# Zero fills, a branch of TensorE, and the order of the score groups in a hybrid attention kernel

## The reference

```python
x = x + attn_a(layernorm(x))   # softmax attention, 16 heads of 8, causal, bias slope[h] * min(k - q, 0)
x = x + ffn(layernorm(x))      # token shift, two mixes, relu squared, sigmoid gate
x = x + attn_b(layernorm(x))   # linear attention with rotary positions
x = x + ffn(layernorm(x))

attn = einsum('bhqd,bhkd->bhqk', Q, K) / sqrt(HD)
attn = where(causal, attn + slopes[:, None, None] * rel, -inf)
out  = einsum('bhqk,bhkd->bhqd', softmax(attn), V) @ W_O.T
```

## Time and profile before

| | us |
|---|---|
| median of 3 runs | 380.14 (379.83 to 380.43) |
| the profiled execution, its own time | 380.15 |
| its span, first to last instruction | 378.4 |
| TensorE busy | 330.1 (87%) |
| ScalarE busy | 293.8 (78%) |
| VectorE busy | 169.4 (45%) |
| GpSimd busy | 62.6 (17%) |
| first score product of the attention starts at | 47.59 |
| last exponential of the attention ends at | 290.8 |

### The profile page before, as it was taken

The page is one execution under the profiler, slowest core; times in us unless marked ns, Lnnn a source line. Parts: engine busy times, 40 slices in busy tenths (PEclk is TensorE's granted clock), DMA queues, the critical chain, the costliest instruction groups (busy, mean ns, idle before and its releaser), DMA issues.

```text
span 378.4 us, 6520 instructions
## 1 busy us (share of the span) xinstructions
PE 330.1 (87%) x2540; PEld 149.6 (40%) x2540; DVE 169.4 (45%) x400; ACT 293.8 (78%) x425; POOL 62.6 (17%) x63
## 2 busy tenths in 40 slices
PE   4814879999999999999999999999999988878795
PEld 2403522323332332322332233223323856868674
DVE  6897511424332422322300331022202779996965
ACT  5201368999999999998899989998999576983771
POOL 8795000003000000000000000000000253720340
PEclk9985958999999999999999999999999999999998
DMA  6220145666400000000000000000001100000002
GB/s 222 58 88 28 60 155 156 194 190 199 136 0 2 0 3 2 0 2 0 2 2 0 3 0 2 0 2 2 0 3 56 57 2 1 3 0 2 1 29 83
DMA packets 13268, 16.47 MB, mean 44 GB/s; under 512 B 1489, under 2 KB 8017, under 8 KB 13137
## 3 DMA queue, kind: packets, MB, share of 16 engines
q1 hardware_dynamic: 13232, 16.01, 13.6%
HBM read 6.56 MB, written 2.62 MB: 24 GB/s over the span
## 4 chain that ended last, share of the span: by engine, by line
PE 57%; DVE 17%; ACT 17%; issue 7%; POOL 1%; DMA 1%; DVEq 0%; ACTq 0%; POOLq 0%
PE ps L998 24%; PE ps L977 17%; ACT probs L488 10%; ACT x L488 5%; DVE probs L264 5%; PE ps L830 4%; PE ps L1007 2%; PE ps L1058 2%; PE ps L843 2%; DVE stats L563 2%; PE ps L825 2%; DVE scr L771 1%; ACT scr L497 1%; DVE ot L685 1%; POOL rstd L412 1%
## 5 line engine op out<-in xcount | busy, mean ns | idle before, releaser
L488 ACT ACTIVATE probs<-ps 128x1024 f32<-128x1024 f32 (+8 forms) x220 | 172.4, 870 | 18.8 <-PE ps L977 17.3
L977 PE MATMUL ps<-qr,kr 64*128 64x512 f32 (+7 forms) x592 | 109.7, 423 | 10.1 <-ACT probs L488 7.3
L998 PE MATMUL ps<-probs,vaug 128*9 128x512 f32 (+9 forms) x880 | 101.3, 509 | 1.0 <-DVE ot L685 0.7
L977 PEld LDWEIGHTS ps<-qr,kr 64*128 64x128 f32 x592 | 49.8, 187 | 117.7 <-ACT probs L488 66.8
L710 DVE TENSOR_TENSOR probs<-probs,cs 128x512 f32<-128x512 f32 x51 | 35.2, 691 | 79.8 <-ACT probs L488 79.8
L488 ACT ACTIVATE x<-ps 128x1024 f32<-128x1024 f32 (+5 forms) x76 | 62.3, 872 | 2.3 <-PE ps L977 2.1
L412 POOL TENSOR_TENSOR rstd<-veps,neghalf 128x4 f32<-128x4 f32 x16 | 17.0, 1064 | 240.9 <-DVE veps L569 240.8
L830 PE MATMUL ps<-w,scr 128*128 128x128 f32 x288 | 35.6, 277 | 2.1 <-DVE scr L773 1.6
L830 PEld LDWEIGHTS ps<-w,scr 128*128 128x128 f32 x288 | 33.9, 192 | 6.2 <-issue 4.3
L998 PE MATMUL ps<-x,vaug 128*9 128x512 f32 (+4 forms) x304 | 34.6, 521 | 0.0
L685 DVE COPY ot<-ps 128x512 f32<-128x512 f32 x16 | 11.1, 691 | 45.8 <-PE ps L998 45.6
(11 more groups left out here) (98 smaller groups left out, 266.1 us busy)
## 6 DMA issues: line engine op xcount, KB each, us to landing
x<-in_x SPq DMA_DIRECT2D x8, 256.0 KB, 4.2
qr<-parts_mid SPq DMA_DIRECT2D x16, 128.0 KB, 2.9
kr<-parts_mid SPq DMA_DIRECT2D x16, 128.0 KB, 3.0
kr<-att SPq DMA_DIRECT2D x8, 128.0 KB, 2.6
qr<-att SPq DMA_DIRECT2D x8, 128.0 KB, 3.2
qr<-parts_last SPq DMA_DIRECT2D x8, 128.0 KB, 3.6
kr<-parts_last SPq DMA_DIRECT2D x8, 128.0 KB, 3.2
out_y<-x SPq DMA_DIRECT2D x4, 256.0 KB, 2.3
```

Of the source, the lines that this page charges most:

```text
L488: nc.scalar.activation(slot[:, 2 * u:2 * u + 2, w0:w1], ps[:, b:b + 2, w0:w1], ACT.Exp).then_inc(exp_done, 1)
L977: ins = nc.tensor.matmul(ps[:, 2 * (n % 3) + v, w0:w1], kr[kb // TPC][a:a + SIDE, j, P * (kb % TPC):P * (kb % TPC + 1)], qr[unit.c][a:a + ...
L998: ins = nc.tensor.matmul(ps[32 * v:32 * v + V1, 6 + unit.lane, w0:w1], vaug[:, kb, V1 * h:V1 * (h + 1)], probs_slot(unit)[:, v, w0:w1], st ...
```

## The change

1. **Zeros.** ScalarE now fills the first half of `qr[1]` too, right behind `kr[0]`. GpSimd fills the other half, and everything else but `kr[1]`, only after DVE has applied the layernorm of slice 2 (`ln1_ready[2]`). SyncE waits for each half by its side.
2. **The first slice.** TensorE turns slice 0 before `gram_products`; `fourth_powers` moves behind the first queries and keys, `sum_of_heads` behind the keys of slice 1. DVE takes the statistics of slices 1 and 2 before `bound(0)`, those of slice 3 behind the first low halves, and `bound(2)` behind its second apply. The warm-up has one product, not two.
3. **Values.** ScalarE takes the values of slices 0 and 2.
4. **The branch.** TensorE reads the flag after slice 2, and `keep_clock` runs 4 products instead of 8, twice. The usual path is now the code right behind TensorE's branch, and the code of the attention and of what follows it, up to slice 3 of the third layernorm, stands a second time in the other block. The two blocks share the code from `turn_ln3(NCH - 1)` on. In `in_turn` the queries and keys of slice 2 now come ahead of `turn_ln3(3)`. SyncE waits for TensorE's `branched` alone.
5. **Groups.** `ORDER` has each group alone, in lane 0.
6. **Constants.** `constant_rows(1, 0)` is issued behind the first three `product_rows`, not ahead of them.

```diff
-WARM_UP = 2
-KEEP = 8
+WARM_UP = 1
+KEEP = 4
...
-        ORDER = (((1, 1), None), ((1, 2), None), ((1, 3), (0, 0)), ((2, 1), (0, 1)), ((2, 2), (0, 2)), ((2, 3), (0, 3)),
-                 ((3, 1), (1, 0)), ((3, 2), (2, 0)), ((3, 3), (3, 0)))
+        ORDER = [((c, g), None) for c, g in ((1, 1), (1, 2), (1, 3), (0, 0), (0, 1), (0, 2), (0, 3), (1, 0), (2, 1), (2, 2), (2, 3),
+                                             (2, 0), (3, 1), (3, 2), (3, 0), (3, 3))]
...
-            for n, m in FIRST:
-                constant_rows(n, m)
+            for n in range(2):
+                constant_rows(n, 1)
             for n, m in FIRST:
                 product_rows(n, m, 0)
-            sp.wait_ge(branched, 2)
+            constant_rows(1, 0)
+            sp.wait_ge(branched, 1)
...
                 rstd_of(LN1, n)
-                if n == 0:
-                    nc.gpsimd.memset(qr[1].bitcast(F32)[:, :, :], 0.0).then_inc(zeroed, 1)
                 if n % 2:
                     ln_apply(nc.gpsimd, pool, LN1, n, xh_a[:, cols(n)])
+            pool.wait_ge(ln1_ready[2], 1)
+            nc.gpsimd.memset(qr[1].bitcast(F32)[:, PAIRS // 2:, :], 0.0).then_inc(zeroed, 1)
             nc.gpsimd.memset(far[:], 0.0).then_inc(pool_ready, 1)
...
-            nc.scalar.activation(kr[0][:, :, :].rearrange("p j t -> p (j t)"),
-                                 neghalf[:, 0:1].broadcast_to([P, PAIRS * CH]), ACT.Copy, scale=0.0).then_inc(first_zeroed, 1)
+            for z, pairs in ((kr[0], PAIRS), (qr[1], PAIRS // 2)):
+                nc.scalar.activation(z[:, 0:pairs, :].rearrange("p j t -> p (j t)"),
+                                     neghalf[:, 0:1].broadcast_to([P, pairs * CH]), ACT.Copy, scale=0.0).then_inc(first_zeroed, 1)
...
                 if n:
                     take_high(n, 1)
+                if n % 2 == 0:
+                    take_values(n)
...
-            for n in range(1, NCH):
-                ln1_stats(n)
-                bound(n - 1)
+            ln1_stats(1)
+            ln1_stats(2)
+            bound(0)
             for s in range(2):
                 low_half(0, s)
+            ln1_stats(3)
+            bound(1)
             ln1_apply(2)
-            take_values(0)
+            bound(2)
             for n in range(1, NCH):
                 low_half(n, 0)
                 low_half(n, 1)
-                take_values(n)
+                if n % 2:
+                    take_values(n)
...
+            turn_ln1(0)
             gram_products()
-            turn_ln1(0)
-            fourth_powers()
             for n in range(NCH):
                 query_or_key(n, 0)
                 if n:
                     turn_ahead(n)
                 query_or_key(n, 1)
                 if n == 0:
+                    fourth_powers()
+                    turn_ahead(n)
+                if n == 1:
                     sum_of_heads()
-                    turn_ahead(n)
                 values(n)
-
-            pe.wait_ge(cb_loaded, 16)
+                if n == NCH - 2:
+                    pe.wait_ge(cb_loaded, 16)
+                    pe.wait_ge(flag_ready, 1)
+                    small = pe.value_load(flag[0:1, 0:1], min_val=0, max_val=1)
             keep_clock(KEEP, 0)
-            pe.wait_ge(flag_ready, 1)
-            small = pe.value_load(flag[0:1, 0:1], min_val=0, max_val=1)
-            with pe.If(small == 0):
+            def larger_scores():
...
+                in_turn(but_first(turn_ln2), but_first(lambda n: mix_k_in(0, n)), lambda n: mix_rv(0, n), None, None, but_last(turn_ln3),
+                        but_last(lambda n: (q_b(n), k_b(n))))
+            with pe.If(small == 1):
+                attention_and_more()
+            with pe.If(small == 0):
+                larger_scores()
+                attention_and_more()
+            turn_ln3(NCH - 1)
+            q_b(NCH - 1)
+            k_b(NCH - 1)
```

83 lines of the change are left out of this document (48 added, 35 removed).

## The result

The changed kernel took 366.46 us (median of 4 executions, 364.77 to 369.90); the kernel before took 380.28 in the same session (4 executions, 379.83 to 383.71). The ratio is 0.963, with a 95% interval of 0.953 to 0.973. The forecast was 359.9 us with a range of 356.0 to 365.5: the direction held, the size did not, and the time lies above the range.

A forecast was written before the change was run, and what follows sets the result against it. It blamed GpSimd's fills holding DVE's apply of slice 2 in the opening, with TensorE and ScalarE both full in the attention. Terms -18.9 - 1.4 - 1.0 + 0.5 - 0.6 + 1.1 = -20.3 from 380.15 gave 359.9 us, range 356.0 to 365.5.

The forecast's parts named there:

- From the apply of slice 2 to the first score: Opening: 13.8 us before, forecast 11.2 as the later of two paths plus 0.3, first score at 28.6.
- The tail: After the attention: TensorE's new jump ahead of turn_ln3(3) costs +1.1 us (0.3 to 4).
- The order: Attention: each group alone instead of mixed costs +0.5 us, bounds -2 to +4.3.
- The 18.9 us: Opening: first score product 18.9 us earlier (16.6 to 21), at 28.6 instead of 47.59.
- path by the rows: Apply to first score: low half after 3.9 us, SyncE's issues near 4, landing 3.0, together 10.9 us.
- path by TensorE's own work: Apply to first score: 13.8 us less clock, fillers and branch hole, plus bound and values copy, 10.7 us.
- The rule weighed: Branch and tail jump: a taken branch outside fetched code stalls; both holes go and return at the jump, shifting 0.8 us.
- The low clock in the first units: First eight units of the attention: half of 1.9 us lost at the lower clock returns, -1.0 us (-1.9 to +2).
- rival (d): Tail jump bites twice: holes of 1.6 and 1.7, then lower clock, +4 instead of +1.1, 362.8 us; chance 0.09.
- (b): Opening: the flag's instruction L604 waits for a GpSimd fill of 3.5 us, giving 363.4 us; chance 0.10.
- (c): Opening: fills hold all of DVE's work, first score at 38, time 369 us; chance 0.04.
- Rival (a): Attention: groups bound by TensorE, order costs +4.3 instead of +0.5, 363.7 us; chance 0.16.

The follow-up runs named there:

- before_third: Kernel of before, no edit, profiled in its short course: 362.46 us; the session's others took 364.16 and, four of them, 379.42 to 383.59.
- before_again: Kernel of before, no edit, profiled again: 381.19 us (3 executions, 380.17 to 381.66), all long.
- b_fills_wait: Kernel of before with GpSimd's memset of `far` and all behind it waiting for the apply of slice 2: 364.18 us (12 executions).
- a_mixed_units: Changed kernel with `ORDER` as in the kernel of before: 364.72 us (362.86 to 367.40, 12 executions).
- a_four_edits: Changed kernel with constant rows in the middle, order of before, jump inside the wait and eight fillers ahead of the jump: 361.13 us (6 executions).
- second trace of the same kernel: Changed kernel once more, no edit: 366.62 us (364.91 to 369.76, 11 executions), the profiled one 367.00.

## Why before has two courses

**Before again, twice.** No edit.

> The kernel of before once more, for a trace of its other course. In 34 further executions it took 361.8 to 366.0 us in 20 and 379.0 to 381.9 us in 14, and nothing between; the trace that the prediction rests on is of one at 380.15. Theory one (VectorE's apply of slice 2 is held, or not): in an execution near 363.5 us that apply, 14.91 us for four instructions beside GpSimd's 6.97 us memset, takes 1.1 us as VectorE's apply of slice 0 does without a memset beside it or up to 7.5 us, the first score comes 14 to 18 us earlier than 47.59 us, and everything from the second group on has the lengths of the trace of before. Theory two (something else differs, such as a transfer that lands late or the clock): the apply takes 14.9 us there too and the time is lost elsewhere.

Measured: 381.19 us (3 executions, 380.17 to 381.66), all long. For the four instructions of the apply of slice 2 the trace gives the duration (ns, shortest/median/longest) and the start of the first and the last, and then DVE's and GpSimd's timelines read:

```profile
L264 DVE TENSOR_SCALAR probs<-x,negmean,rstd x4: 328/7524/15041, 18.3 to 33.5; 128x128 f32<-128x128 f32 x4
```

```profile
18.27 15.61 DVE L264 TENSOR_SCALAR probs<-x,negmean,rstd 128x128 f32<-128x128 f32 x4
```

```profile
18.61 0.82 POOL L434 MEMSET far<- 128x864 f32 x1
```

The first instruction takes 15.04 us, from 18.27 to 33.31; the second stands behind it and ends with it; the last two take 0.33 each. GpSimd's memset of `far` starts at 18.61, and four fills of 3.5 us follow without a gap, up to 33.2. The prediction had the instructions let in one by one between two fills. They are not: the first waits for all five memsets. By these rows its start lies 0.34 us ahead of the first memset, in the trace of the prediction 0.37 behind it (18.85 against 18.48), and it is held in both.

> The kernel of before again, since the trace taken last fell in its long course too (381.19 us, the apply of slice 2 held from 18.27 to 33.88 us, GpSimd's memset of the tile far beginning at 18.61). Theory one (the apply is caught by the memsets, or gets through ahead of them): in an execution near 363.5 us the apply begins at 17.5 us or earlier, takes 1.1 us and is over when that memset begins; the first score stands 14 to 18 us earlier than 47.59. The rest has the lengths that the trace at 380.15 us shows. Theory two: the apply begins as late as in the long course and is not held, so what holds it is something else.

Measured: one execution at 362.46 us, which was the profiled one, one at 364.16, four from 379.42 to 383.59. The short course on DVE and on GpSimd:

```profile
15.39 0.27 DVE L603 TENSOR_REDUCE largest<-ps 1x1 f32<-1x128 f32 x1
15.70 0.14 DVE L604 TENSOR_SCALAR flag<-largest 1x1 int32<-1x1 f32 x1
15.77 1.27 DVE L581 SCALAR_TENSOR_TENSOR att<-ps,att 128x512 f32<-128x512 f32 x2
16.96 1.09 DVE L264 TENSOR_SCALAR probs<-x,negmean,rstd 128x128 f32<-128x128 f32 x4
```

```profile
18.59 0.81 POOL L434 MEMSET far<- 128x864 f32 x1
```

The apply is over at 18.05, half a us ahead of the memset. In the long course it began at 18.85, 0.4 us after it. What made it 1.9 us later is TensorE. First the short course (`before_third`), then the long one of the profile before:

```profile
12.58 1.88 PE L843 MATMUL ps<-probs,w 128*128 128x512 f32 x4
14.39 0.38 PE L863 MATMUL ps<-cs,fourth 128*1 128x128 f32 x2
```

```profile
13.10 3.62 PE L843 MATMUL ps<-probs,w 128*128 128x512 f32 x4
16.65 0.58 PE L863 MATMUL ps<-cs,fourth 128*1 128x128 f32 x2
```

The same four products take 1.88 us or 3.62 (592 ns each or 1061), the full or the half level. The sum over heads behind them, which DVE's reduction and all behind it wait for, starts at 14.4 or at 16.65. (The clock's column says 1.00 for both: no change is on record until 11.3 and 17.8 us, and only the durations tell which level the start has. The other long trace, `before_again`, has a record: the half level from 12.28 to 15.70 us, and the sum at 16.27.)

**More or less work for TensorE at the start.**

```
-WARM_UP = 2
+WARM_UP = 4
```

> The kernel of before with four products of 384 columns in TensorE's opening in place of two. Theory one (which course an execution of before takes is decided by when TensorE's clock has risen: in the short one the four products of query and key of slices 0 take 592 ns each and the sum over heads starts by 14.7 us, in the long one 1061 ns each and it starts at 16.3 to 16.7, so the apply of slice 2 comes 1.3 to 1.9 us later and meets GpSimd's memset): two more products, 1.3 us at the half level, fill the 0.9 us that TensorE idles at 9.4 us, the clock rises by 11.5 us in nearly every execution and nearly all take the short course, 362 to 366 us. Theory two (the course is decided by the arrival of the weights or of x): about half stay near 380 us.

Measured: 365.13 us (363.54 to 367.89), 12 executions, none long; 1.0036 of the short course (1.0003 to 1.0069). The four products take 1.88 us at 12.86, and the apply begins at 17.25.

```
-WARM_UP = 2
+WARM_UP = 0
```

> The kernel of before without those two products, the opposite step. Theory one (the clock decides the course): TensorE has done less by 11 us, the clock rises late, the four query and key products take 1061 ns each, and nearly all executions take the long course, 379 to 384 us. Theory two: about half stay near 363.5 us. A third outcome would be that the products start 1 us earlier without the two ahead of them, and enough so that even at the half level the sum over heads is there in time; then nearly all are short and the clock is right only in part.

Measured: 380.48 us (378.61 to 382.32), 6 executions, all long. TensorE's timeline shows the four products at 13.05 taking 3.62 us, and DVE's apply 14.48 us from 18.71. In the same session 15 executions of before were short and 8 long. Theory one in both: the level that the clock has during these four products decides the course.

**GpSimd's later fills wait.**

```
+            pool.wait_ge(ln1_ready[2], 1)
             nc.gpsimd.memset(far[:], 0.0).then_inc(pool_ready, 1)
```

> The kernel of before with one wait added on GpSimd: the memset of the tile far and all behind it begin only after VectorE's apply of slice 2, the early fill of query slice 1 stays where it was. Nothing on VectorE or TensorE changes. Theory one (the long course is that apply caught by these memsets and nothing else; the clock only sets when it begins): the apply takes 1.1 us in either clock, no execution near 380 us is left, those with the late clock end 1 to 2 us above the others, and all lie between 361.5 and 367 us. Theory two (a late clock costs the 16 us in another way): a part stays near 380 us. Beside the kernel whose fill of slice 1 waited as well (370.69 us) this one tells what that fill's lateness cost: some 6 us.

Measured: 364.18 us (362.25 to 366.91), 12 executions, none long. With the fills away from the apply nothing else remains of the 16 us.

**The apply ahead of the bound's wait.**

```
             for n in range(1, NCH):
                 ln1_stats(n)
+                if n == NCH - 1:
+                    ln1_apply(2)
                 bound(n - 1)
...
-            ln1_apply(2)
             take_values(0)
```

> The kernel of before with one edit on VectorE: the apply of slice 2 stands ahead of the step that waits for TensorE's sum over heads (and of the flag and the two low halves), as in the changed kernel, and no longer behind them; GpSimd's fills stay where they were. Theory one (the long course is this apply caught by the memsets that begin at 18.5 us): it begins at about 15.7 us and ends by 17, so no execution near 380 us is left, and the times are those of before's short ones, 362 to 365 us. Theory two (GpSimd's memsets hold whatever VectorE runs beside them): a part of the executions stays long.

Measured: 364.30 us (361.55 to 366.38), 12 executions, none long. The apply runs from 15.66 for 1.12 us. In the profiled execution the four products took 3.62 us, so the clock was late there and the course short all the same (363.5 us of span): for the long course the clock matters only through the moment of the apply. Either edit alone takes the long course away at no cost to the short one (ratios 1.0001, 0.9975 to 1.0027, and 1.0006, 0.9970 to 1.0043). The changed kernel pays 0.8% for the same.

**GpSimd's fill of query slice 1 late as well.**

```
-                if n == 0:
-                    nc.gpsimd.memset(qr[1].bitcast(F32)[:, :, :], 0.0).then_inc(zeroed, 1)
...
+            pool.wait_ge(ln1_ready[2], 1)
+            nc.gpsimd.memset(qr[1].bitcast(F32)[:, :, :], 0.0).then_inc(zeroed, 1)
             nc.gpsimd.memset(far[:], 0.0).then_inc(pool_ready, 1)
```

> The kernel of before with one edit: GpSimd fills query slice 1 with zeros only after VectorE has applied the normalisation to slice 2 (in the changed kernel GpSimd's half of it waits for the same). Theory one (the long executions of before are those in which the apply of slice 2 is held beside the memset): no execution near 380 us is left, the applies take 1.1 us each, and the times are those of before's short ones or some us longer, since the fill ends later: it would start at about 16 to 18 us, take 3.5 us for the whole slice, and the copies into it could not go out before about 21 us; 362 to 366 us. Theory two (the long executions have another cause): a good third of the executions stay at 379 to 382 us.

Measured: 370.69 us (369.17 to 372.01), 6 executions, none long, above the expected 362 to 366. The fill now ends at 20.75, and SyncE's queue holds the constant rows of query slice 1 ahead of everything else, so all other rows go out behind it. TensorE's timeline shows the bill:

```profile
38.86 1.65 PE L977 MATMUL ps<-qr,kr 64*128 64x512 f32 x6 [10.14 <-DMA kr<-parts_mid]
```

A full late fill, with the queue in its old order, thus costs 6.5 us against `b_fills_wait`. The changed kernel halves this fill and also moves the constant rows back in the queue; no run tells which of the two keeps it from this loss.

## Where the changed kernel stays above the forecast

**The constant rows.** In SyncE's program, with `product_rows` calling `between` ahead of its middle parts:

```
-            for n, m in FIRST:
-                product_rows(n, m, 0)
-            constant_rows(1, 0)
+            product_rows(0, 1, 0)
+            product_rows(1, 0, 0, lambda: constant_rows(1, 0))
+            product_rows(1, 1, 0)
```

> The changed kernel with one edit on SyncE's queue: the four copies of the constant rows of query slice 1 are issued in the middle of that slice's product rows, before the two of the middle parts, rather than behind the product rows of key slice 1. Theory one (the constants are late): they were issued from 24.27 to 25.6 us and landed 5.6 us later, and TensorE stood 2.84 us for them ahead of its first score at 31.26 us. Now they are issued by about 20.7 us, the last transfer to go out is a copy of key slice 1's product rows, issued by 25.6 us, and the first score comes at 28.4 to 29.0 us. The clock then has no reason to fall at 30.55 us, and the first eight units take 12.7 us, not 14.28: 2.5 plus 1.5, so 4 us less than the changed kernel, 361 to 364 us. Theory two (the landing is slow because of what else moves on the 16 DMA engines, not because of its place in the queue): another transfer lands last at about 31 us, the first score stays within 0.5 us of 31.26, and the time stays at 366.5.

Measured: 364.20 us (360.71 to 366.32), 12 executions; 2.4 below the changed kernel. In the trace the first score comes 12.5 us after the apply (17.13 to 29.66), before it was 14.9 (16.33 to 31.26), and it still waits, now for product rows:

```profile
29.66 1.65 PE L998 MATMUL ps<-qr,kr 64*128 64x512 f32 x6 [2.02 <-DMA kr<-parts_mid]
```

The time lies just above theory one's 361 to 364, and so does the first score with its 28.4 to 29.0. Theory two falls. The landing is longer than the 3 us reckoned with: the last copy was issued by 25.1 and the score came 4.6 later. The half level stayed in this execution, at 28.9 for 10.2 us; of the gain of 4 us only the rows' part was there.

**The order.** `ORDER` as in before, the rest as changed.

> The changed kernel with the order of before: the units of seven groups spread among those of seven others; all else as changed. Theory one (the order costs): from the second group on ScalarE takes 226.5 us as in the trace of before, not 228.1, and the time is 1 to 2 us below the changed kernel's. Theory two (the order costs nothing): ScalarE's stretch from the second group on stays at 228 and the time at 366.5; the 1.7 us were then the price of something else, such as GpSimd's memsets or the clock. Theory three (the order gains, as the numbers of steps of few columns would have it): slower by 1 us or more.

Measured: 364.72 us (362.86 to 367.40), 12 executions, 1.9 below. From the second group to the last exponential, the mixed order and the groups one by one (`a_mixed_units`, then the changed kernel):

```profile
45.50:272.09 226.59, 217.97 (x1746) 69.17 (x1742) 60.38 (x108) 213.11 (x281) 3.52 (x1) 1.00 0.10 30
```

```profile
46.44:274.57 228.13, 220.55 (x1750) 70.10 (x1746) 61.05 (x111) 212.84 (x281) 3.52 (x1) 1.00 0.10 30
```

ScalarE's busy time is nearly the same in both; TensorE's is 2.6 us more. The groups cost 1.5 us. Theory one.

**The order alone, in the kernel before.** `ORDER` as changed, the rest as before.

> The kernel of before with the changed order of the units alone: groups one by one. Theory one (the order costs 1.5 to 1.7 us, as the changed kernel with the old order showed: 226.6 us from the second group on against 228.1): its short executions are 1.5 to 2 us above those of before, so 365 to 366 us, and its long ones near 382. Theory two (the order matters only with the late first rows of the changed kernel): within 0.5 us of before in both courses.

Measured: 382.55 us (381.69 to 383.50), 6 executions, all long, against 380.7 for the long ones of before. The 1.9 us agree. That all six were long, with an opening that is the same, may be chance; 13 of 24 executions of before were long in that session, and no run tells.

**The jump inside a wait.** TensorE leaves its block one step ahead of `turn_ln3(1)`, where it stood 2.41 us for ScalarE (`in_turn` takes a first and a last step for this):

```
+            middle = (but_first(turn_ln2), but_first(lambda n: mix_k_in(0, n)), lambda n: mix_rv(0, n), None, None, turn_ln3,
+                      lambda n: (q_b(n), k_b(n)))
...
-                in_turn(but_first(turn_ln2), but_first(lambda n: mix_k_in(0, n)), lambda n: mix_rv(0, n), None, None, but_last(turn_ln3),
-                        but_last(lambda n: (q_b(n), k_b(n))))
+                in_turn(*middle, stop=6)
...
-            turn_ln3(NCH - 1)
-            q_b(NCH - 1)
-            k_b(NCH - 1)
+            in_turn(*middle, start=6)
```

> The changed kernel with TensorE's jump over the second path moved forward in the tail, from ahead of the last slice's turn to ahead of the second slice's turn (behind the first one's), where TensorE stood 2.41 us for ScalarE's normalised slice at 303 to 306 us; the stages ahead of and behind it are in the order of before again. Theory one (the jump's hole is hidden by a wait): the row of that wait stays near 2.4 us, no further hole of 1.4 us stands in the tail, the last slice's turn comes ahead of the third slice's products again, DVE's wait of 1.6 us ahead of the following products is back, and the tail (last exponential to the end, 91.6 us in the changed kernel) gets 0 to 0.6 us shorter by that. If the jump's hole is also what lets the clock fall at 317.27 us, another 1.7 us: 364 to 366.5 in all. Theory two (the clock falls in the tail by chance, jump or no jump): as many stretches at the half level in the tail as with the changed kernel, three in its profile, and a time within 0.7 us of 366.5. Theory three: the hole begins only when the wait ends, because what is behind the jump is read when it is reached and the wait stands behind it; then the row of the wait is 3.8 us and the time 1 to 1.5 us above the changed kernel's.

Measured: 364.54 us (362.82 to 366.37), 12 executions, 2.1 below. TensorE's timeline:

```profile
307.30 0.63 PE L842 MATMUL ps<-cs,scr 128*128 128x128 f32 x4 [2.48 <-ACT scr L512]
307.76 1.99 PE L847 MATMUL ps<-w,scr 128*128 128x128 f32 x16
...
320.28 1.13 PE L847 MATMUL ps<-w,scr 128*128 128x128 f32 x8 [1.62 <-DVE scr L790]
```

The wait is 2.48 us and no other hole follows, so the jump is hidden and theory three falls. The tail took 88.8 us instead of 91.6, with the half level once (at 343.4), not three times.

**TensorE's branch as before.**

```
-            with pe.If(small == 1):
-                attention_and_more()
             with pe.If(small == 0):
                 larger_scores()
-                attention_and_more()
+            attention_and_more()
```

with the last slice's turn and products back in `in_turn`. The load of the flag stays ahead of slice 3's products.

> The changed kernel with TensorE's branch as before: the usual path lies behind the skipped code, and there is no jump in the tail. Theory one: the tail gets 2.8 us shorter, as it did when the jump lay inside a wait (88.8 us from the last exponential to the end in place of 91.6: two stretches at the half level, 3.4 us, and the hole of 1.42 us, less what DVE's wait gives back), and at the branch up to 1.6 us comes back as a hole, hidden as far as TensorE waits 2 to 3.7 us for the rows of slice 1 there anyway: 363.0 to 365.5 us. Theory two (the hole at the branch is not covered by that wait, since the code after the first score has to be read too): a hole of 1.4 us behind the first six products as in the trace of before, and 365 to 366.5 us.

Measured: 363.77 us (361.54 to 364.48), 12 executions, 2.9 below (in another session; against the short course of before the ratio is 0.9994 in place of 1.0078); the tail took 88.5 us. Behind the first scores there is 0.71 us of waiting for ScalarE, and no hole:

```profile
30.49 0.97 PE L996 MATMUL ps<-qr,kr 64*128 64x512 f32 x6 [1.45 <-DMA qr<-qc]
32.17 1.60 PE L996 MATMUL ps<-qr,kr 64*128 64x512 f32 x4 [0.71 <-ACT probs L503]
```

## Together

**Three edits**: constant rows in the middle, order of before, jump inside the wait.

> The changed kernel with three edits together: the constant rows in the middle of the product rows, the order of before, and the jump moved into the wait ahead of the second slice's turn. Alone their medians were 2.4, 1.9 and 2.1 us below the changed kernel's 366.62 in the same session. Theory one (the three are at different places and add up): 360.2 us, 359.5 to 361.5. Theory two (most of each was the same clock stretch that fell away or another draw of it): 362 to 364 us.

Measured: 358.85 us (358.56 to 361.01), 6 executions; ratio 0.989 (0.984 to 0.994) to the short course of before, the shortest median of all kernels here. TensorE's timeline at the first scores:

```profile
27.78 0.60 PE L901 MATMUL ps<-cb 128*128 128x256 bf16 x4
28.31 0.96 PE L998 MATMUL ps<-qr,kr 64*128 64x512 f32 x6
29.99 0.50 PE L998 MATMUL ps<-qr,kr 64*128 64x512 f32 x2 [0.71 <-ACT probs L505]
```

The first score stands at 28.31, with no wait, and the first eight units take 12.33 us at the full clock. The single gains, 2.4, 1.9 and 2.1, make 6.4; together it is 7.8, against the changed kernel of another session. The median lies below theory one's 359.5 to 361.5. In this execution the clock did not fall in the first units; two of the six, 360.80 and 361.01, have lower mean clocks (0.983 and 0.980, the others 0.988).

**The branch as before, without the wait that hid it**: constant rows in the middle, order of before, branch of before.

> The changed kernel with the constant rows in the middle of the product rows, the order of before, and TensorE's branch as before (the usual path behind the skipped code, no jump in the tail). Theory one (the branch moved a hole of 1.6 us that now, with the rows there in time, is no longer hidden by a wait for them): a hole of 1.4 to 1.9 us at or behind the first scores, as in the trace of before, and 360.0 to 361.0 us, 1.4 to 2 us above the kernel with the jump inside a wait (358.85). Theory two (the code is there in time either way): 358.3 to 359.2 us.

Measured: 359.43 us (358.56 to 362.87), 11 executions. The first score waits 0.26 us for rows, the next step 0.71 for ScalarE, as with the jump; no hole. Against 358.85, from another session, this is no difference that can be told. Theory two: the hole of before does not come back with the old branch. What the old branch and the new one share here is the load of the flag ahead of slice 3's products, where the kernel before had it behind the last fillers.

**Fillers ahead of the jump**: the three edits and

```
                 in_turn(*middle, stop=6)
+                pe.wait_ge(gate_ready, 2)
+                keep_clock(8, low(1))
```

> The three edits together (constant rows in the middle, order of before, jump inside the wait) and a fourth: eight filler products on TensorE ahead of the jump, in the wait of 2.41 us for ScalarE's normalised slice, behind which the clock fell to the half level for 3.41 us at 300.35 us in the trace with three edits. Theory one (that idle stretch is what lets it fall): eight fillers take some 1.04 us of it as the eight do later in the tail, the jump's hole of 1.4 us still fits beside them, the stretch at the half level is gone and the time falls by up to 1.7 us, to 357.2 to 358.8. Theory two (the fillers push the hole behind the end of the wait, or the clock falls all the same): 358.9 to 360 us.

Measured: 361.13 us (357.64 to 363.05), 6 executions. The wait ahead of the turn is 1.59 us and the clock stays full there, in this execution; but a hole of 0.82 follows one turn later, so the fillers take part of the wait that had hidden the jump, and the half level came at 30.75 for 6.8 us in the opening, which the fillers do not touch. The median is above both theories' ranges. Against the short course of before in their own sessions the four edits stand at 0.990 and the three at 0.989: no gain can be told. The execution at 357.64 had a mean clock of 0.994, so next to none of either.

**Fillers at the branch too**: `KEEP = 8` in place of 4.

> The four edits together, and eight fillers of 256 columns on either side of the first product behind the branch as the kernel of before has them, in place of four. With four of them the trace of the four edits showed the half level from 30.75 to 37.58 us, the first eight units taking 14.05 us in place of 12.3, and its six executions spread from 357.64 us (mean clock 0.994) to 363.05 (0.980). Theory one (the idle stretches between the last values and the first scores, 0.73 and 0.29 us and then 0.2 to 0.7 between the first score steps, let the clock fall in some executions; fillers cover the first of them): most executions keep it, the median falls to 358 us or below, at 0.5 us more for the four fillers that no wait covers. Theory two (the clock is lost on the waits for ScalarE between the first score steps, which the fillers don't touch): the same spread, and a median of 360.5 to 361.5 us.

Measured: 362.95 us (360.21 to 364.65), 12 executions. The half level came at 33.9 us, behind the first score steps, and in the tail at 303.6 for 6.8 us although the fillers stood there; a hole of 2.25 us, up to 305.2, followed the jump. The median is above theory two's 361.5. Its reading of the clock holds as far as it goes: neither set of fillers keeps it. What decides whether it falls with the rows in time stays open.

## Why the prediction was right or wrong

**The steps that failed.** Three terms of the sum were mis-sized. From the apply of slice 2 to the first score it put 11.2 us, and 14.9 passed: the constant rows left last, the rows took longer to land than reckoned, and TensorE's own work ran in part at the half level. The tail was put at +1.1 and came to +4.5. The order was put at +0.5 and cost +1.7. Moving the rows, moving the jump and putting the order back took 2.4, 2.1 and 1.9 us off the median, and all three together gave 358.85 us. That this lies so near the forecast of 359.9 is in part luck, since the forecast's terms for the clock did not come as worked out.

**The apply of slice 2: right, for a reason in part wrong.** Forecast end 17.4, measured 16.33. The fills had held it. But one instruction waited through five memsets. The Trainium skill, SBUF — State Buffer, section Who interferes with whom, says that whoever of VectorE and GpSimd issues first has the shared ports for its whole instruction. The trace of the prediction agrees, where the memset of `far` starts 0.37 us ahead of the apply; in `before_again` the apply's record starts 0.34 us ahead of the memset, and it is held all the same. That a waiting VectorE instruction is not let in between back-to-back fills is this case's 15.04 us.

**The base: the step that no part of the sum had.** The 18.9 us were the gain over the long course. The trace held the warning: the apply began 0.4 us behind the memset's start, behind products that ran at the half level. Over the short course (29.99) the changed kernel has hardly a gain at the first score: 31.26, 29.71. This does not explain the miss, since forecast and result both stand against the long course. But it makes the direction luck: beside short executions of before the same kernel is 0.8% slower.

**From the apply to the first score: too short.** Forecast 11.2, measured 14.9, so the first score came at 31.26 and not at 28.6; in the second trace of the same kernel it was 13.5 and 29.71. On the path by the rows two terms failed. The landing of 3.0 us from the earlier trace rows is a median; here 5.6 passed between the last issue and the product. And the constant rows, last in the queue, were counted as part of one run of issues and not as the thing waited for. With them in the middle it was 12.5, with 4.6 behind the last issue. The path by TensorE's own work, put at 10.7, was too short as well: in the four traces in which it waited at most 0.3 us for rows, the first score came 12.0 to 12.5 us after the apply. It was reckoned at the full rate, but 3.4 us of it, from 16.9 or 17.1 on, ran at the half level, which is worth 1.7, and TensorE stood 0.73 us for DVE's last copy of values, put at 0.3. There the first score stood at 28.3 to 28.8, near the forecast.

**The hole behind the branch: gone, as forecast, but not by the new branch.** The first exponentials have no hole; with the branch of before they have none either. The load of the flag, put at 0.8 us, left no idle time on TensorE in its new place. The rule weighed, the Trainium skill's Runtime: NRT & Kernel Launch, Instruction fetch mechanics, would have the stall return at that branch. It did not, in two traces, and the jump in the tail has its hole (1.42 to 2.21 us in four traces). Why the one jump is covered and the other not, no run tells; that the flag is loaded early is the likely cause and was not tried by itself.

**The low clock in the first units.** Forecast -1.0 and -1.4 for the hole, together -2.4; measured -1.74 (16.02 to 14.28). The half level lasted 10.24 us as before, and the mean clock was 0.70 in place of 0.68, so of the -1.0 next to nothing came. It stood there in all six traces of changed kernels with a wait of 1.4 to 3.7 us for the rows. But it also came behind a wait of 0.29 us (`a_four_edits`) and in the short course of before behind none, so the wait alone does not decide it.

**The order: +0.5 forecast, +1.5 to +1.9 measured**, inside its bounds of -2 to +4.3. Groups (2, 0), (2, g) and (3, 2) took the 12.9, 19.9 and 27.3 us that were worked out, to 0.3 us. The mis-sized term is (3, 1) with (1, 0), put at 25 + 11.3: they took 26.16 + 11.85, which is what they took mixed (38.05). The other lines of `ORDER` each took 0.1 to 0.4 us more than mixed, 1.7 together.

**End of the attention: right.** The first turn of the tail stage came 0.5 us sooner after the last exponential; 0.6 was forecast.

**The tail jump: the hole was sized well, its company was not.** From `turn_ln3(1)` to the first sum of keys went 18.42 us in place of 14.46. Of the 4.0, 3.4 are half of two stretches of 3.42 us at the half level. The other 0.5 is the jump's hole of 1.42 and a wait of 0.68 for ScalarE's copy, less DVE's wait of 1.63, which is gone. Later 0.8 came back, and a third stretch cost 1.3. So it is +4.5 in place of +1.1, and with the end of the attention +3.9 in place of +0.5.

Not all of this is the jump's. The first stretch begins at 307.03, ahead of the jump and behind a wait of 2.41 us that the kernel before has too; the short course of before falls to the half level there as well (304.9). The third is found in two edited kernels of before without the jump (341.2 and 342.5). The second goes with the jump: it stands at 315.6 to 317.3 in all four traces with the jump in this place, and in none of the six others of changed kernels. So rival (d) came in part, as one hole and one stretch, about 1.7 us. From the end of the last exponential itself the tail took 90.4 to 91.7 us in the four traces, and 88.2 to 88.9 in five of the six others; the sixth, with the hole of 2.25 us behind its fillers, took 92.1.

**Rivals (b) and (c) fall**: the flag's instruction took 0.14 us, the low halves 0.69, with a memset beside them. The Trainium skill's SBUF — State Buffer, Who interferes with whom, says of tensor_scalar that it can contend when its operands meet certain conditions; with one element it did not here. **Rival (a)** gave +4.3 and fell too.

**The signs named.** The apply under 2 us, no idle time over 2 us from 8 to 28 us, the flag's 0.14 us and a hole ahead of `turn_ln3(3)` all came. The first score at 31.26 is past the 31 us that were to show the forecast wrong; in the second trace it is not. From the first to the last exponential it took 242.6 us as before, not 240.7.

In the profiled pair the miss of 8.1 us is: first score 2.6, the step from there to the first exponential 0.3, first units 0.7, order 1.2, tail with the end of the attention 3.4.

## What to carry to other kernels

A stall between two engines whose starts lie within a us of each other is a race, and one trace shows one side of it: take several executions of the kernel before, and see whether its times fall into groups, before the stall is priced as a gain. Here one wait on GpSimd or one moved line on VectorE ends the long course and costs nothing, while the larger change is 2.8 us longer: rows behind other rows in a queue, short groups that the mixing had hidden, a jump where TensorE had work. If code must be jumped over, put the jump where the engine waits anyway, and leave that wait empty: with fillers in it holes of 0.82 and 2.25 us were seen again.

## What the runs showed of the hardware that was not expected

- A VectorE instruction that meets GpSimd's memsets waits for all that follow without a gap: 15.04 us for one that otherwise takes 0.33. Beside GpSimd's own apply the same four instructions took 1.09 us together.
- The level of TensorE's clock around 13 to 17 us decided 17 us at the end. With two more products at the start 0 of 12 executions were long, with two fewer 6 of 6.
- The changed kernel spread by 5 us in one session (364.9 to 369.8), and the mean granted clock from 0.980 to 0.966 with it.
- Where TensorE waited for the rows of the opening, its first score came 4.4 to 6.5 us after SyncE's last issue for it (nine traces); the median landing of the middle parts over the kernel is 2.9 to 3.2.
